# Transposing the attention probabilities as whole 128-row blocks or as pairs of 64-row halves

## What is computed

```python
x = x + layernorm(attn(layernorm(x)))     # 16 heads of 64, causal, k and v by way of a rank-128 latent
x = x + layernorm(ffn(layernorm(x)))      # 8 experts, each token goes to one (argmax), width 512
# attn, per batch and head:
att = softmax(where(causal, q @ k.T * 64**-0.5, -inf))
y   = att @ v ;  out = concat(y) @ w_out
```

## Time and profile before

| | |
|---|---|
| median of 3 runs | 1368.81 us (1368.3 to 1368.97) |
| the profiled execution, its own time | 1369.18 us |
| its span, first to last instruction | 1366.2 us |
| mean granted TensorE clock | 0.982 |
| PE, PEld, DVE, ACT, POOL busy | 96%, 88%, 87%, 79%, 67% |
| attention slots | 32 to 1137 us; experts after that |

### The profile page before, as it was taken

The page is one execution under the profiler, slowest core; times in us unless marked ns, Lnnn a source line. Parts: engine busy times, 40 slices in busy tenths (PEclk is TensorE's granted clock), DMA queues, the critical chain, the costliest instruction groups (busy, mean ns, idle before and its releaser), DMA issues.

```text
span 1366.2 us, 34597 instructions
## 1 busy us (share of the span) xinstructions
PE 1307.4 (96%) x9120; PEld 1201.3 (88%) x9120; DVE 1188.7 (87%) x4712; ACT 1082.8 (79%) x3186; POOL 908.9 (67%) x1343
## 2 busy tenths in 40 slices
PE   6999999999999999999999999999999997699993
PEld 5999999999999999999999999999999996588782
DVE  4899999999999999999999999999999884699993
ACT  5988888888888888888888888888888884466661
POOL 3566666666666666666666666666666564288886
PEclk9999999999999999999999999999999998899997
DMA  5000000000000000000000000000000002122220
GB/s 211 5 9 13 12 12 12 12 12 12 12 12 12 12 12 12 12 12 12 11 9 8 11 12 12 12 12 12 12 12 8 8 10 76 42 62 59 60 61 8
DMA packets 38501, 31.83 MB, mean 23 GB/s; under 512 B 4882, under 2 KB 35734, under 8 KB 38080
## 3 DMA queue, kind: packets, MB, share of 16 engines
q1 hardware_dynamic: 31696, 21.47, 5.2%
q0 software_dynamic: 4656, 8.81, 1.9%
q10 hardware_dynamic: 2112, 1.11, 0.3%
HBM read 20.35 MB, written 12.07 MB: 24 GB/s over the span
## 4 chain that ended last, share of the span: by engine, by line
PE 82%; DVE 8%; issue 3%; POOL 3%; DMA 2%; ACT 1%; ACTq 0%; SPq 0%; POOLq 0%; DVEq 0%
PE psS L579 19%; PE psZU L643 13%; PE psZU L628 13%; PE psP L606 12%; PE psZU L631 7%; PE psT L595 5%; PE psT L597 4%; PE psT L596 4%; DVE ff L367 2%; DMA xin<-x 2%; DVE wup_s L384 1%; POOL out L446 1%; DVE on L393 1%; DVE gg L402 1%; PE psM L671 1%
## 5 line engine op out<-in xcount | busy, mean ns | idle before, releaser
L1097 POOL TENSOR_TENSOR prob<-prob,rinv 128x256 f32<-128x256 f32 (+1 forms) x512 | 412.9, 828 | 333.7 <-DVE rinv L858 330.4
L725 ACT ACTIVATE prob<-nscore,nmax 128x128 f32<-128x128 f32 (+1 forms) x1024 | 450.8, 445 | 3.1 <-DVE nmax L840 3.1
L840 DVE CUSTOM_DVE_ANT_0 nscore<-psS,mask 128x128 f32<-128x128 f32 (+1 forms) x1024 | 319.8, 349 | 0.2 <-PE psS L579 0.2
L697 ACT ACTIVATE t_hi<-psT 128x512 fp32r<-128x512 f32 x256 | 153.2, 598 | 151.3 <-PE psT L597 151.3
L827 DVE TENSOR_TENSOR t_lo<-psT,t_hi 128x512 fp32r<-128x512 f32 x256 | 176.5, 689 | 81.7 <-ACT t_hi L697 79.5
L849 DVE TENSOR_TENSOR p_lo<-psP,p_hi 128x768 fp32r<-128x768 f32 x256 | 243.3, 951 | 3.8 <-ACT p_hi L697 3.8
L697 ACT ACTIVATE p_hi<-psP 128x768 fp32r<-128x768 f32 x256 | 208.3, 814 | 6.3 <-PE psP L606 4.1
L606 PE MATMUL psP<-ident,prob 128*128 128x128 f32 x1536 | 209.3, 273 | 0.4 <-DVE p_lo L849 0.4
L863 DVE TENSOR_TENSOR z_lo<-psZU,z_hi 128x512 fp32r<-128x512 f32 x256 | 175.1, 684 | 28.4 <-ACT z_hi L697 14.4
L725 ACT ACTIVATION_READ_ACCUMULATOR prob<-nscore,nmax 128x1 f32 x1024 | 195.0, 190 | 0.0
L579 PE MATMUL psS<-t_lo,xt_hi 128*128 128x256 f32 (+1 forms) x512 | 194.3, 380 | 0.0
(11 more groups left out here) (168 smaller groups left out, 3295.7 us busy)
## 6 DMA issues: line engine op xcount, KB each, us to landing
fin<-routed_rows SPq DMA_DIRECT2D x40, 136.0 KB, 2.2
wx<-ffn_w SPq DMA_DIRECT2D x2, 2058.0 KB, 11.7
xin<-x SPq DMA_DIRECT2D x32, 128.0 KB, 2.2
xres<-x SPq DMA_DIRECT2D x32, 128.0 KB, 2.1
out<-res,fin POOLq DMA_INDIRECT x80, 2.3
routed_rows<-padr ACTq DMA_DIRECT2D x4, 272.0 KB, 4.3
routed_rows<-padr SPq DMA_DIRECT2D x4, 272.0 KB, 5.2
wup_s<-wup SPq DMA_DIRECT2D x1, 1024.0 KB, 5.0
```

The costliest lines, as they stand in the source:

```text
L697: cp = lambda o, i: nc.scalar.activation(o, i, ACT.Copy)
L725: last = nc.scalar.activation(prob[:, pb, h, a:z], nscore[:, (s - lag) % 2, h, a:z], ACT.Exp, bias=nmax[:, pb, h, q:q + 1], scale=-1.0, ac ...
L840: last = v.tensor_tensor_reduce(nscore[:, n1, h, a:z], psQ[q][:, h, :], mask[:, a:z], -1.0, -MASKED, ALU.add, ALU.min, nmax[:, p1, h, q:q ...
L1097: last = g.tensor_tensor(pr, pr, rinv[:, p2, :, q:q + 1].broadcast_to([P, 2, z - a]), ALU.mult)
```

## The change

Each 128x128 block of prob is transposed as two blocks of 64 rows: the one in partitions 0 to 63, with the upper left 64x64 of `ident`, gives the columns 64n to 64n+63 of psP's first bank; the one in partitions 64 to 127, with the lower right 64x64, gives the same columns of the second bank. The halves alternate. Twelve transposes take the place of six. The last of each half raises pt_ready, so ACT waits for twice the count. The wait for norm_ready is made with `wait_apart`, the value for p_split is computed in a register ahead of it. ACT's and DVE's instructions that empty psP keep their 128x768 elements; they now write (and DVE reads p_hi) through a view that puts the 64-column runs of the two banks back in their places.

```diff
+        psPh = psP[:, :, 0:384].rearrange("p e (n c) -> p e n c", c=64)
+        def by_half(buf, b):
+            return buf[:, b].rearrange("p h (k e c) -> p e (h k) c", k=3, e=2)
@@ PE, slot
-                    pe.wait_ge(S["norm_ready"], g0 + s - 3)
+                    freed = g0 + s - 4
+                    if not isinstance(freed, int):
+                        pe.compute_val(freed)
+                    wait_apart(pe, S["norm_ready"], g0 + s - 3)
                     if live(5):
-                        pe.wait_ge(S["p_split"], g0 + s - 4)
-                    for h in range(2):
-                        for k in range(3):
-                            last = nc.tensor.transpose(psP[:, h, k * P:(k + 1) * P],
-                                                       prob[:, s % 4, h, k * P:(k + 1) * P], ident[:])
-                    last.then_inc(S["pt_ready"], 1)
+                        pe.wait_ge(S["p_split"], freed)
+                    for n in range(6):
+                        h, k = n // 3, n % 3
+                        for e in range(2):
+                            half = slice(64 * e, 64 * e + 64)
+                            last = nc.tensor.transpose(psP[:, e, 64 * n:64 * n + 64],
+                                                       prob[half, s % 4, h, k * P:(k + 1) * P], ident[half, half])
+                            if n == 5:
+                                last.then_inc(S["pt_ready"], 1)
@@ ACT, slot
-                    act.wait_ge(S["pt_ready"], g0 + s - 3)
+                    act.wait_ge(S["pt_ready"], 2 * (g0 + s - 3))
-                    cp(p_hi[:, s % 2], psP[:, :, 0:384]).then_inc(S["p_hi_done"], 1)
+                    cp(by_half(p_hi, s % 2), psPh).then_inc(S["p_hi_done"], 1)
@@ DVE, slot
-                    v.tensor_tensor(p_lo[:, s % 2], psP[:, :, 0:384], p_hi[:, s % 2].bitcast(F32),
+                    v.tensor_tensor(by_half(p_lo, s % 2), psPh, by_half(p_hi, s % 2).bitcast(F32),
                                     ALU.subtract).then_inc(S["p_split"], 1)
```

## The result

The changed kernel takes 1384.09 us (median of 4 runs, 1383.32 to 1384.8) against 1368.55 us before: ratio 1.0116, interval 1.0098 to 1.0133. It is **slower by 15.5 us**; 1381 was forecast. The profiled execution has a span of 1381.4 us against 1366.2.

The account below looks back on a forecast made before the run. PE's pace was taken to bound the slots. Per slot 0.645 (pairs) + 0.147 (way in) + 0.145 (way out) = 0.937 against 0.89 us, +12 us over 256 slots, giving 1381 us; range 1366 to 1450.

Parts of the forecast that it names:

- The halves run in pairs: PE's transposes: twelve halves go as six pairs 0.057 us apart instead of 0.109; gain 0.245 us a slot.
- Going into 64-row work: PE, before the first half transpose: 0.21 us to the first load plus 0.057 for it, against 0.12; +0.147 us.
- Coming out of it: PE, from the last half transpose to the first whole-array score load: 0.145 us more a slot.
- The sum: PE, last matmul of T to second score matmul: 0.937 against 0.89 us, +0.047 a slot, +12 us for 256 slots.
- The waits: PE's sequencer: one more wait and up to two register instructions are covered by its lead and cost nothing.
- emptying psP: ACT's p_hi and DVE's p_lo, writing runs of 64 with the same elements: no cost.
- no price for the turns: Rival, PE's transposes: entering and leaving 64-row work costs nothing, only the gain stays; -63 us, 1306 us; chance 0.12.
- a half takes as long as a whole: Rival, PE's transposes: pairs form but stay 0.109 us apart; +79 us, 1448 us; chance 0.13.
- the halves take turns: Rival, PE's transposes: halves do not overlap, eleven distances of 0.057 us; +97 us, 1466 us; chance 0.06.

Follow-up runs that it names:

- the run with everything but the split: Six whole transposes as in the kernel before, with the change's added waits, register instruction and p_hi/p_lo views: 1368.52 us, ratio 0.9996 against the kernel before.
- the run of two groups: Changed kernel with its twelve half transposes in two groups of six, the second behind the first three score matmuls: 1466.27 us, ratio 1.0709 against the kernel before.
- the run of upper halves first: Changed kernel with the six upper-half transposes issued first, then the six lower ones, instead of alternating: 1425.98 us, ratio 1.0411 against the kernel before.

## Why the prediction was right

The direction, the mechanism and the time were right, by the steps that it names.

- *The halves run in pairs*: right. Loads and matmuls start in twos, 3 ns apart where 10 were allowed for. The pair's distance was mis-sized: 0.062 for 0.057. What streams is not the limit, as was said, but some 5 ns on top of the load were left out. Five distances: +0.025 us a slot, of which a way in of 0.206 for 0.21, the 3 ns for 10 and a few ns more take 0.012 back.
- *Going into 64-row work*: 0.21 and 0.057, as taken from the setup.
- *Coming out of it*: 0.15 for 0.145, and 0.22 for 0.23 to the second score matmul. The size holds, its working does not: by 0.055 of streaming and 0.09 of emptying a half with 32 columns would have needed less, and it needs the same 0.151.
- *The sum*: over 192 slots in the middle the interval is 0.950 us on average against 0.894 before (0.937 against 0.89 was forecast), +0.056 and not +0.047: 14.3 us in 256 slots for the forecast's 12.
- *The waits* and *emptying psP*: nothing, as the run with everything but the split shows directly.
- *Not foreseen*: in one slot of eight PE waits for DVE's one-hot rows (L676, L688 after). That wait shrinks by about the same 0.05 (from the last matmul of U to the next it is 0.20 and 0.285 us in turn before, 0.15 and 0.23 after), so such a slot is no longer than before, and 32 x 0.05 = 1.6 us come back. And the single gap adds 2.6. 14.3 - 1.6 + 2.6 = 15.3, and the spans differ by 15.2. That these two unforeseen terms nearly cancel is luck.

Of the rivals, *no price for the turns* falls with the run of two groups, *a half takes as long as a whole* and *the halves take turns* with the timeline. The rule of the Trainium skill on loads ("TensorE: Matmul & The Clock Gate", section "LDWEIGHTS (loading the stationary operand)": 107 ns for 128 columns) does not hold for the loads of fp32 transposes: the pairs are 0.062 apart. It does hold for the score loads behind the turn, 0.11 apart. That on the change of tiling mode ("TensorEngine Tiling (Array Packing)", section "Key Properties") agrees with the two turns, which cost about 0.147 us going in and 0.145 coming out.

What carried the prediction was that the setup of the same kernel already does 64-row work: four rows of it held both turns. Priced from the steady slots alone, the change would have looked like a gain of 63 us.

## What to carry to other kernels

Work on parts of the array pays only in runs long enough to cover the way in and the way out, here 0.29 us together. Six blocks save 0.23 (five distances of 0.047), so they lose; by the same figures it would take eight to come out ahead, an estimate, and splitting only some of the six is worse than splitting all or none. Put such work side by side in one place, alternate the parts in the program, and look for the price of the turns in timelines between groups, since busy times and mean durations do not hold it. Before splitting, ask which of load and stream sets the distance: splitting the rows halved what streams here and left the load at its 0.057.

## What the runs showed of the hardware beyond that

- Instructions for the two halves of the array overtake each other. Already in the setup both halves' L549 start before any L550, though the program has the first half's L550 ahead of the second half's L549. In the run of upper halves first, the lower half starts before the fourth upper one does. Whether a count on the last instruction alone would tell that both halves are done was not tested; the changed kernel counts one for each half.
- The lead of one half over the other was three transposes, in 255 of 256 blocks of that run; what sets it was not tried.
- fp32r brings the distance of whole transposes from 0.109 to about 0.086 us, and not to the 0.06 at which the first two follow each other.
